# Four-stage sequence kernel on one core: output bias as a TensorE product, two VectorE steps on ScalarE, SSM preparation placed later, instruction order refitted

## What is computed

```python
x = x + L0_attn(ln(x))   # A: linear attention, 16 heads of 8, decayed state
x = x + L0_ffn(ln(x))    # B: mixture of 8 experts, top 2, 352 hidden
x = x + L1_attn(ln(x))   # C: conv, SiLU, selective scan with 16 states, gate, Wout + bout
x = x + L1_ffn(ln(x))    # D: mixture of 8 experts, top 2, 128 hidden, and a shared expert
```

```python
# A: decay of the state; sigmoid(y) is computed as 0.5 * tanh(y/2) + 0.5
lc = sigmoid(tanh(x @ cs_w1.T + cs_b1) @ cs_w2.T + cs_b2)
lam = clip(sigmoid(decay_params) * (1.0 + 0.2 * lc), 0.0, 0.9995)
# C: step size; softplus(y) is computed as max(y, 0) + log(1 + exp(-|y|))
dt = softplus(x @ Wdt + bdt)
# C: the end
return x_ssm * z @ Wout + bout
```

## Time and profile before

| what | value |
|---|---|
| median of three runs | 1718.2 us |
| lowest of them | 1715.0 us |
| the profiled execution | 1725.16 us |
| its span, first to last instruction | 1723.4 us |
| mean granted TensorE clock | 0.912 of full |
| PE, PEld, DVE, ACT, POOL busy | 80%, 54%, 79%, 54%, 56% |
| ACT_TABLE_LOADs | 163, of 1283 ns each |

### The profile page before, as it was taken

The page is one execution under the profiler, slowest core; times in us unless marked ns, Lnnn a source line. Parts: engine busy times, 40 slices in busy tenths (PEclk is TensorE's granted clock), DMA queues, the critical chain, the costliest instruction groups (busy, mean ns, idle before and its releaser), DMA issues.

```text
span 1723.4 us, 29120 instructions
## 1 busy us (share of the span) xinstructions
PE 1375.9 (80%) x9192; PEld 927.2 (54%) x9192; DVE 1369.6 (79%) x2543; ACT 936.7 (54%) x1637; POOL 965.6 (56%) x571
## 2 busy tenths in 40 slices
PE   0778899999899985997989667978948875767688
PEld 0335377875567564675566434665614643534355
DVE  0689879798998895968999669489879588758846
ACT  0231354647765763567554675578456574585451
POOL 1000505288186493864867787740188677764776
PEclk9898899999999997999899669989979887888799
DMA  8620346676887585887778768899669788987953
GB/s 272 195 67 2 100 139 175 181 188 212 281 242 236 167 290 171 261 225 232 238 243 197 203 216 265 225 314 308 197 217 279 188 220 269 239 221 240 282 126 69
DMA packets 293905, 361.58 MB, mean 210 GB/s; under 512 B 33753, under 2 KB 234361, under 8 KB 293497
## 3 DMA queue, kind: packets, MB, share of 16 engines
q1 hardware_dynamic: 251512, 328.12, 61.2%
q0 software_dynamic: 42240, 31.61, 10.1%
HBM read 306.09 MB, written 55.50 MB: 210 GB/s over the span
## 4 chain that ended last, share of the span: by engine, by line
PE 30%; issue 20%; DVE 19%; POOL 10%; DMA 8%; ACT 7%; SPq 5%; POOLq 0%; DVEq 0%; ACTq 0%
POOL x L887 6%; PE bank L992 5%; DVE arena_c L1513 3%; PE bank L943 3%; PE bank L1064 3%; DVE arena_a L1440 3%; PE bank L952 3%; DMA arena_c<-bc_rows 3%; POOL rows L868 3%; DVE arena_c L1499 2%; DVE arena_c L1508 2%; PE bank L938 2%; DMA xg<-rows 2%; DVE arena_a L1451 2%; PE bank L910 2%
## 5 line engine op out<-in xcount | busy, mean ns | idle before, releaser
L887 POOL DMA_INDIRECT x<-outs,slot_idx x240 | 488.8, 2037 | 171.9 <-DMA outs<-yrow 88.3
L868 POOL DMA_INDIRECT rows<-xrow,slot_idx x240 | 356.9, 1487 | 85.8 <-issue 62.2
L992 PE MATMUL bank<-arena_c,ident 128*128 128x512 f32 x512 | 272.5, 663 | 34.9 <-DVE arena_c L1499 34.7
L1513 DVE TENSOR_TENSOR_SCAN arena_c<-arena_c 128x1024 f32<-128x1024 f32 x128 | 297.2, 2324 | 3.7 <-ACT arena_c L1271 3.3
L910 PE MATMUL bank<-xT_ring,mix 128*128 128x128 f16 (+1 forms) x1296 | 244.9, 227 | 59.6 <-DVE mix L1689 26.9
L912 PE MATMUL bank<-xT_ring,mix 128*128 128x128 f16 (+1 forms) x1296 | 244.3, 226 | 0.0
L911 PE MATMUL bank<-xT_ring,mix 128*128 128x128 f16 (+1 forms) x1296 | 244.2, 226 | 0.0
L1064 PE MATMUL bank<-mix 128*128 128x128 f32 (+1 forms) x1296 | 188.2, 291 | 40.9 <-ACT yrow L1316 19.7
L1064 PEld LDWEIGHTS bank<-mix 128*128 128x128 f32 (+1 forms) x1296 | 169.9, 201 | 74.8 <-issue 67.5
L910 PEld LDWEIGHTS bank<-xT_ring,mix 128*128 128x128 f16 (+1 forms) x1296 | 140.6, 108 | 106.0 <-issue 64.1
L1508 DVE TENSOR_TENSOR arena_c<-arena_c 128x1024 f32<-128x1024 f32 x128 | 160.4, 1256 | 26.6 <-DMA arena_c<-bc_rows 16.2
(11 more groups left out here) (223 smaller groups left out, 2366.1 us busy)
## 6 DMA issues: line engine op xcount, KB each, us to landing
arena_c<-bc_rows SPq DMA_DIRECT2D x256, 512.0 KB, 5.8
mix<-weights_B SPq DMA_DIRECT2D x168, 352.0 KB, 4.0
mix<-weights_B SPq DMA_DIRECT2D x168, 192.0 KB
xg<-rows SPq DMA_DIRECT2D x156, 129.0 KB, 4.2
outs<-yrow SPq DMA_DIRECT2D x156, 128.0 KB, 4.7
mix<-weights_D SPq DMA_DIRECT2D x144, 128.0 KB, 3.0
mix<-weights_D SPq DMA_DIRECT2D x144, 64.0 KB
rows<-mix SPq DMA_DIRECT2D x3, 2580.0 KB, 13.1
```

The costliest lines, as they stand in the source:

```text
L868: pool.indirect_dma_start(out=xs_d[q % ROW_SETS], out_offset=bass.IndirectOffsetOnAxis(ap=slot_idx[:, q % RJ, c, j:j + 1], axis=0), in_=xr ...
L887: pool.indirect_dma_start(out=x[:, b, j, :], out_offset=None, in_=y_d[q], in_offset=bass.IndirectOffsetOnAxis(ap=slot_idx[:, q % RJ, c, i ...
L992: last = pe.matmul(bank[C_BANKS[h]][:], ident[:], half(hb[:, n % RR, :], h), start=(n == 0), stop=(n == NS - 1))
L1513: dve.tensor_tensor_scan(hb[:, n % RR, :], dA[:, n % RDA, :], hb[:, n % RR, :], 0.0, ALU.mult, ALU.add).then_inc(c_scan.sem, 1)
```

## The change

Four things are done.

1. The bias: `c_bias` goes from POOL, with its chain "B" and its semaphore. `bout` is loaded as one row of 128 instead of 128 equal rows. In `c_out` each of the four products of a half is followed by a product of a row of ones with `bout_row`, accumulated into the same place.
2. `a_clip`'s multiply and add goes from VectorE to ScalarE, behind the Tanh of the same half, which it waits for.
3. The max(y, 0) of dt goes from VectorE to ScalarE as a Relu from PSUM, directly behind the Abs of the same half. It waits until the batch before has used dt.
4. `ORDER` is another string, of 4893 letters (8 of B and 16 of C fewer). Its first letters are 23 A: `ready("C")` and `conv_taps` are now behind attention's batch 0, in the middle of batch 1.

```diff
-                return [("C{}.dt{}".format(*args), C_BANKS[args[1]], "c_dve")]
+                return [("C{}.dt{}".format(*args), C_BANKS[args[1]], "c_act")]
...
-            sp.dma_start(bout_all[:], t["bout"].rearrange("d o -> o d").broadcast_to([P, D])).then_inc(s_w["C"], 16)
+            sp.dma_start(bout_row[:], t["bout"].rearrange("d o -> o d")).then_inc(s_w["C"], 16)
...
-            def c_bias(b):
-                if b == 0:
-                    wait_weights(wt, "C")
-                wt.wait_ge(normed["C"].sem, normed["C"].at(b, TT))
-                pool.tensor_tensor(x[:, b, :, :], x[:, b, :, :], bout_all[:].unsqueeze(1).broadcast_to([P, TT, D]), ALU.add).then_inc(
-                    c_biased.sem, 1)
...
-                    last = pe.matmul(o[:, rows], half(w, h)[:, rows], Wout[:], start=True, stop=True)
+                    pe.matmul(o[:, rows], half(w, h)[:, rows], Wout[:], start=True, stop=False)
+                    last = pe.matmul(o[:, rows], ones[0:1, :], bout_row[:], start=False, stop=True)
...
                 if name == "lam":
+                    if b == 0 and h == 0:
+                        wt.wait_ge(s_lamc, 2)
                     read(n, act.activation(half(lam, h), psum(n), ACT.Tanh, bias=half_b2[:], scale=0.5))
+                    U.wait_empty(wt, n)
+                    act.activation(half(lam, h), half(lam, h), ACT.Identity, bias=lam_add[:], scale=lam_mul[:]).then_inc(a_lin.sem, 1)
...
+                n = f"C{b}.dt{h}"
+                act.activation(half(sp_abs, h), psum(n), ACT.Abs, bias=col["bdt"]).then_inc(c_sp.sem, 1)
+                if b:
+                    wt.wait_ge(w_done.sem, w_done.at(b - 1, 1))
+                    wt.wait_ge(c_dA.sem, c_dA.at(b - 1, NS))
+                read(n, act.activation(half(dt, h), psum(n), ACT.Relu, bias=col["bdt"]))
...
-                if s == "C":
-                    wt.wait_ge(c_biased.sem, c_biased.at(b, 1))
...
-                for h in range(NH):
-                    U.wait_empty(wt, f"A{b}.lam{h}")
-                    dve.tensor_scalar(half(lam, h), half(lam, h), lam_mul[:], lam_add[:],
-                                      ALU.mult, ALU.add).then_inc(a_lin.sem, 1)
...
-            def c_dt_in(b, h):
-                n = f"C{b}.dt{h}"
-                wt.wait_ge(c_sp.sem, c_sp.at(b, h + 1))
-                read(n, dve.tensor_scalar(half(dt, h), psum(n), col["bdt"], 0.0, ALU.add, ALU.max))
```

The first lines of the two orders:

```diff
-    "AACACAAAAAAAAAAAAAAAAWAAAAAAWWoAAsAoWAAosAAwqAwsWwokAPkqsowqwWsAwoqAqwsoqAswokAqsCoqsAoqsoAwskwowqAqWoAswswq"
+    "AAAAAAAAAAAAAAAAAAAAAAAWAWWAAoAskkoAPWAosAqskoqWAWwkAsoAqswqowqAwWsoAqsowwqsAoAqwsowqAksAwokqwkskoqWoswsoqAA"
```

More of the change, by code:

```diff
@@ new lines @@
+    "sAqLVXTZSwUVNwUMeRPeLTAUAVAULMULTCVAUAAPKMVLRZKPVAPNUUReZNLeTUAAAZPVMALAPKUAVPUPAALAAXAPAVATVULKNASASAZULUoL"
+    "sAUNVkoVRMkRsSPAUSKUoZqRqTLPUAMsoMXwXkTsVwXLAPVoXULUqskXAqkoUqKwSLsPPkeAwoVVeATwosMqAULwUALsoskqKXPKUoqNVRAw"
+    "kwoANAPessowUUVSZqsqVosqPLwwPqZMRTUPeoSAsLwZqKwVAUeosqNARSALAoPUPUwPwTqMswAqLKVwVwPAULUZRAVNPAeALTUMSNPKPUAV"
+    "ULPPAUZPTVMeKNPSAPZSPPUVGPPRLAPLeUPRAAANVTPRAGAeUPZAGMKNUAGSLAVAPRZAALPUAVTLeSUMKVRANTMGAeXAUUoUAVLGSZLNkVoK"
+    "sRksoAULqUAKTMseUGowZqwAsVLNkqkZToUkVLsqRAoUMLUVAVqoGwskUXAKoTUeXLsekSUVwAsMkNKqLoUAwTMCCLVqsUoXwUSCqAwowCVA"
@@ new lines @@
+    "sqCUoCqLsACVCCCsUosCRCCoXCqsZXAowCCCCLUACNCCCwACSLCXVKXXwZCAqSsToCwXwqVXqqNsbUceAXUACXqRMZLdwwUwVbwxdwNScbAK"
+    "ATZAAAAMeAdhxAbXPpcAhxAAAAALAAUAeAALpNbbAxhVAAdcXAPepKXUcVdyZULoPyAhRNSxPsRdbdhAoVKRZxsTMyNdeRocpASTUhpoUbqS"
+    "cVxMLyKesUqPwRTPLAcPwUVyLpZPUbkkUhALoskKVNpVMUqZbUsTPxoPxNcUhbMPRLPLyPdSPqVqAUGKVPephyodUcLLTexMwSUVshAVUNZK"
+    "wTLqoUxUZRdNkKswSbVpTdMULkeARSVqRMeoLUSdkwshUAykZoLKscbVAoNqUwGqwVULkATpswxyosUbTMAUVLpcdeoqyxGKANVhZUbLqUso"
+    "sdwwMxZAsyeNKVoLURLVGARUUTeqhVwLZMcRwodKcqTwMspqVSqbNyUweUpATULsGNZKULAVwVqewUMcLUyhAcZApwNyUPARSVxRAZGLAePT"
@@ L121 @@
+    "ESTuSZlNUMZvEnnuLVNalEGGZTGGuvMlUELnnvFeFIVSaJJGFIEZINOJOSFFOGIFIOGOFGOIFOFFOIIFOGIFGOFOIOIFGOFGOFQGOJGJQQJQ"
+    "QGJQJQJOJQIJGIJQQJIGQIQGJIQJQJQQQ"
 )
@@ L424, in ssm @@
             steps += [(m, b, n, h) for n in "uz" for m in ("c_in", "c_read") for h in range(NH)]
-            steps += [(n, b, h) for n in ("c_dt", "c_dt_abs", "c_dt_max") for h in range(NH)]
+            steps += [(n, b, h) for n in ("c_dt", "c_dt_abs") for h in range(NH)]
             steps += [(n, b, h) for n in ("c_bc", "c_bc_read") for h in range(NH)]
@@ L455, in build @@
             "C": [("ready", "C"), ("conv_taps",), ("conv_weights",), ("conv_scaled",)] + [st for b in range(B) for st in ssm(b)],
-            "B": [("c_bias", b) for b in range(B)],
             "D": [("d_load",)],
@@ L891, in m_gather @@
                         compute_op=ALU.add).then_inc(gathered[i] if c else gathered_first[j], 16)
-            program({"top": top, "d_rstd": d_rstd, "c_bias": c_bias, "ready": ready, "s_rstd": inverse_deviation, "m_rstd": m_rstd, "m_scatter": m_scatter, "m_gather": m_gather})
+            program({"top": top, "d_rstd": d_rstd, "ready": ready, "s_rstd": inverse_deviation, "m_rstd": m_rstd, "m_scatter": m_scatter, "m_gather": m_gather})
         @block.tensor
@@ L1251, in c_dt @@
             def c_dt(b, h):
-                act.activation(half(sp_abs, h), psum(f"C{b}.dt{h}"), ACT.Abs, bias=col["bdt"]).then_inc(c_sp.sem, 1)
+                n = f"C{b}.dt{h}"
[4 more added lines that the diff above has]
+                read(n, act.activation(half(dt, h), psum(n), ACT.Relu, bias=col["bdt"]))
             def c_bc(b, h):
@@ L1705, in _ @@
                      "m_stats": m_stats, "a_clip": a_clip, "s_shift": shifts, "m_shift": m_shift, "a_outer": outer, "a_scan": scan, "a_qs": a_qs, "a_add": a_add,
-                     "conv_taps": conv_taps, "conv_scaled": conv_scaled, "c_dt_max": c_dt_in, "c_rate": c_rate, "c_dbx": c_dbx, "c_scan": c_scan_of,
+                     "conv_taps": conv_taps, "conv_scaled": conv_scaled, "c_rate": c_rate, "c_dbx": c_dbx, "c_scan": c_scan_of,
                      "c_prod": c_prod_of, "c_gate": c_gate, "s_add": s_add, "m_centre": m_centre, "m_choose": m_choose,
```

81 lines of the change are left out of this document (34 added, 47 removed).

## The result

The changed kernel is 0.7% slower, not 2.3% faster. One of the 20 runs of the kernel before took 7331.3 us and is left out of the ratio.

A forecast was written before the change was run, and what follows sets the result against it. No engine was full throughout: a dead stretch at the start, held by C's preparation, then a dense middle. 1725.2 - 33.5 (start) - 6 (moved steps) = 1685.7; the median lies 7.0 below the profiled run, so 1679 us, range 1651 to 1707.

The forecast's parts named there:

- The start: First 50 us: C's preparation no longer holds up the first batch of stage A; -33.5 us, carried to the end.
- The wait ahead of `scale`: VectorE at the start, waiting for POOL's reduction over the partitions: 3 us taken, between 0 and 15.9.
- the stall of 0.5 us: Alternative for the wait ahead of `scale`, from about 6 us of POOL code loading; the sum 2.5 us lower.
- The moved steps: Clip and Relu from VectorE to ScalarE, bias from POOL to TensorE: weighed to -2.2 us, taken as -6.
- the 99% stretch: Window from 400 to 500 us, VectorE working 99 of 100 us; its saving was to count in full there.
- the rival at 1651: VectorE bounds the middle and its 34.6 us saving counts in full: 1651 us; full or half, chance 0.14.
- The order: The new order string, nearly the same per engine: 0 us, with 12 us to either side.
- The rival of SP's queue: Expert weight loads come late behind waits on SP and TensorE stands: 1757 us at 20 blocks, chance 0.06.
- The bias products: 64 added TensorE products in C's output stage: 2.0 us a batch, 16.1 in all, weighed to +4.8.
- The upper bound of 16.1: Most that the new TensorE bias products could add on the path, in us; the lower bound was 0.
- the added work is on the path: Rival: new products delay each batch's last addition, ScalarE's additions delay dt, nothing given back: 1710 us, chance 0.13.
- The last sign that I named: First 190 us shorter by 34 and the span not: the middle took it back, windows there show which engine.

The follow-up runs named there:

- without the moves: The kernel before with only stage C's preparation steps moved behind attention's first batch: 0.9801 of before, 1687.5 us.
- After: The changed kernel with all four edits, against the kernel before: 1.0072 of before, 1732.4 us.
- the old order: The order of the kernel before with only stage C's preparation moved; with all edits and alternating one-row bias products it measured 1.0040 of before.
- with 128 rows: The changed kernel with its bias products made from the identity and a full 128-row bias tile, still alternating: 0.9826 of before, 1689.9 us.
- the kernel with 32 rows: The changed kernel with its bias products over 32 rows, each holding bout/32, instead of one row: 1.0050 of before.
- the two 128-row kernels of the old order: Order of before with C's preparation moved, ScalarE moves, 128-row bias products: alternating 0.9761, one 512-column product per half 0.9792 of before.

## Why the prediction was wrong

**The start: right.** The forecast was `outer` at 25.5 us and it came at 24.64. The staged weights ended a wait of 4.95 us and the peaks began at 15.19, 0.8 us ahead of the earliest that I gave. The first `keep` was to come at 73.4 at the earliest:

```profile
71.66 6.07 SPq L717 DMA_DIRECT2D weights_B<-mix  x4
```

It came at 71.66, 1.7 us ahead of that bound, right behind the last load, issued from 70.91 to 71.53. SP's own loads still held it, as said. The wait ahead of `scale`, put at 3 us, was nothing: the result was there at most 40.35 - 35.05 = 5.3 us after `floor` started, so the stall of 0.5 us that the prediction works out beside it isn't seen either. (The bound of 21.6 us that it reads from the earlier trace rows counts from the reduction's start; from the end of `floor` it is 21.75, which its sum does use.) The whole term was put at -33.5 us. Alone it measured 1720 x 0.0199 = 34 us. How close this is was partly luck: with `outer` 38.4 us earlier and no wait ahead of `scale`, the same sum gives -37.4.

**The moved steps: prices right, worth too high.** The estimate for Identity was 823 ns, the one for Relu 688:

```profile
L1229 ACT ACTIVATE arena_a<-arena_a,lam_add,lam_mul 128x512 f32<-128x512 f32 x16 | 13.0, 814 | 0.5
L1253 ACT ACTIVATE arena_c<-bank,cols 128x512 f32<-128x512 f32 x16 | 11.0, 690 | 0.0
```

The table loads are 164, as worked out. But weighing VectorE's saving by its share of the chain and then rounding up for the 99% stretch gave -6 us, and the runs show none: 0.9801 without the moves, 0.9795 with them. The intervals leave room for some us either way; the whole saving of 34.6 us (the rival at 1651) would have been 0.960 and is excluded. VectorE at 99% of a window did not mean that work taken from it comes back as time. Whether VectorE's saving was worth nothing, or was worth something that ScalarE's 20 us took back, no run separates.

The prediction's count of VectorE's saving also left a term at nothing: it says that VectorE never waited for the bias, which is so, and not that POOL's additions made VectorE's own instructions longer, 12 to 16 us in all (1344.9 against 1332.8 and 1348.3 against 1332.5, with and without them). Whether they came back as time the runs can't tell: 0.9790 without POOL's additions against 0.9846 with them, and 0.9792 against 0.9795, with overlapping intervals in both pairs.

**The order: right.** 0 with 12 us to either side. After against the same edits in the old order is 1.007 against 1.004; with the bias on POOL 0.985 against 0.980; with 128 rows 0.983 against 0.976. If anything the refit costs 5 to 11 us by these ratios, but in each pair the intervals overlap. The rival of SP's queue, at 78 us, is excluded by the same pairs.

**The bias products: the step that failed.** The term that was mis-sized is the price of the new TensorE products. I put them at 2.0 us a batch, 16.1 in all, and weighed them down to 4.8 because other work would hide most of it. Measured, they add (63.3 - 16.1) / 8 = 5.9 us a batch inside the stage, 47.2 in all, and after is 47.5 us longer than the kernel without a bias. The price rested on one sentence, "a contraction of 32 took 617 ns where 128 took 615". That row is true, and the Trainium skill ("TensorE: Matmul & The Clock Gate", Why this matters for your kernels) says the same of a single product of 32 rows. But it is the mean of products of 512 columns, which come in pairs. One such pair in the kernel before, with a product of 128 rows behind it (and others ahead):

```profile
121.33 1.98 PE L934 MATMUL bank<-arena_a,cs_w 32*128 32x512 f32 x4
123.23 1.13 PE L943 MATMUL bank<-arena_a,Wv 128*128 128x512 f32 x2
```

The pair takes 1.90 us from start to start, and so does the pair of 128 rows ahead of it (from 119.43): at 512 columns the change of the row count is not seen. The new products have 128 columns and take turns one by one, which neither a row of before nor that page prices, and the kernel with 32 rows measured 0.41 us a product for it. The sum was right for another kernel. How the cost depends on the columns no run tells. With 128 rows the stage measured 32.5 / 8 = 4.1 us, where 2.0 + 2.0 was forecast. Its products cost 1689.9 - 1684.9 = 5.0 us against no bias (the intervals overlap), where 4.8 was forecast, and nothing against the bias on POOL. Their stages add 32.5 - 18.2 = 14.3 us, so by the medians other work hides 9 of them. It doesn't hide what comes on top: after's stages take another 30.8 us, and its span is 43 us longer. That the lower clock makes up the rest is argued above. The upper bound of 16.1 was called a bound though it was only a price taken from rows of wider products and of equal neighbours.

The rival "the added work is on the path" had the place right and ended at 1710 because it used the same price. With 47.2 us for the products in place of 16.1 its sum would have been 1679 + 6 + 0.6 x 72.7 = 1729, beside the measured 1732. That agreement is partly luck: 25.5 of the 72.7 us are ScalarE's, and the runs put the moves as a whole, with what they save on VectorE, at nothing.

The last sign that I named was the right one: the first 190 us were shorter by the amount forecast and the span was not. TensorE's busy time then said on which engine to look.

## What to carry to other kernels

Price an added matmul by a row with the same columns in which it stands between the same neighbours, not by the mean of its shape: in fp32, with 128 columns, products of 1 or 32 rows taking turns with products of 128 rows take nearly twice as long as with equal row counts, and the unchanged neighbours pay too. If a bias must go through TensorE, give it the row count of what is around it, or group it so that the count changes rarely. And before moving work off an engine because a window shows it 99% busy, make a run that takes the work away without giving it to another: here 18 and 34 us less of VectorE's work, with 19 to 20 us more on ScalarE, bought nothing. When a step leaves POOL, look at VectorE's longest instructions before: some of them may be waiting inside for POOL's.

## What the runs showed of the hardware

- A change of the row count between 128 and 1 or 32, from one fp32 product of 128 columns to the next, costs about 0.2 us: 0.41 us from start to start at full clock, against 0.22 with 128 rows throughout. 1 and 32 rows behave alike. Between products of 512 columns no such cost is seen (1.90 us for a pair of 32 rows and for one of 128, in the kernel before). The next weight load starts late instead of in the shadow of the product in front. Why the chip does so is not shown.
- TensorE's granted clock was 0.57 to 0.87 in the 10 us behind 23 of the 24 alternating stages of three kernels, with the engine busy by its records for 7.3 to 10.0 us of the 10; behind all other stages it was 0.83 or more. What in those stages brings it down is not shown.
- The result of POOL's reduction over the partitions was in use 5.0 us after the reduction started (35.35 to 40.35), without any wait; before, all that was known was 21.6.
- A VectorE scan of 128x1024 that met POOL's addition over 128x1024 took up to 5.41 us, where its median is 2.28. In the three kernels with that addition whose scans were compared (before, the old order with the moves, after with the bias on POOL) the longest took 5.41, 5.41 and 4.32 us; in four without it (after, no bias, and the two 128-row kernels of the old order) none took above 2.35. Why the one holds up the other is not shown.
